# Weight-only products of two late stages computed at the start of the 16-head attention

## What is computed

```python
x = x + tanh(g_xattn[0]) * L0_xattn(ctx, ctx, layernorm(x))   # 16 heads of 16
x = x + tanh(g_ffn[0])   * L0_ffn(layernorm(x))               # 4 experts, each row to one
x = x + tanh(g_xattn[1]) * L1_xattn(layernorm(x), ctx, ctx)   # one head of 256
x = x + tanh(g_ffn[1])   * L1_ffn(layernorm(x))               # product-key memory

# L1_xattn: each of Q, K, V is a weight plus a product of rank 16
Q = query @ Q_weight.T + (query @ Q_A.T) @ Q_B.T
# L1_ffn: batch norm over all rows, queries, similarity with 2 x 8 x 64 keys, top 8
xn = (x - mu) * rsqrt(var + eps) * gamma + beta
sim = einsum(xn @ w_q.T, keys)
```

## Time and profile before

| | us |
|---|---|
| median of 3 runs | 3782.14 (3780.43 to 3783.98) |
| the profiled execution | 3779.93 |
| its span | 3778.3 |
| PE busy | 3467.6 (92%) |
| DVE busy | 2495.0 (66%) |
| ACT busy | 1560.8 (41%) |
| POOL busy | 226.7 (6%) |

### The profile page before, as it was taken

The page is one execution under the profiler, slowest core; times in us unless marked ns, Lnnn a source line. Parts: engine busy times, 40 slices in busy tenths (PEclk is TensorE's granted clock), DMA queues, the critical chain, the costliest instruction groups (busy, mean ns, idle before and its releaser), DMA issues. The chain is left out here.

```text
span 3778.3 us, 67015 instructions
## 1 busy us (share of the span) xinstructions
PE 3467.6 (92%) x21900; PEld 2037.8 (54%) x21900; DVE 2495.0 (66%) x5808; ACT 1560.8 (41%) x2718; POOL 226.7 (6%) x251
## 2 busy tenths in 40 slices
PE   8958999999999999867986999995999999999999
PEld 5631222222222222256873454544889888888898
DVE  4538877888788788461103344435888888888885
ACT  4525766767667677711221222211222222223221
POOL 0022000000000000020000000000000000000000
PEclk9978999999999999978997999996999999999999
DMA  5676445446445444051112122213000000000000
GB/s 218 229 210 96 61 68 79 60 66 81 60 69 72 67 63 57 5 189 48 38 51 78 46 91 64 64 40 147 9 12 10 11 12 10 11 10 11 12 10 9
DMA packets 144210, 240.30 MB, mean 64 GB/s; under 512 B 22808, under 2 KB 100224, under 8 KB 143488
## 3 DMA queue, kind: packets, MB, share of 16 engines
q1 hardware_dynamic: 134768, 220.67, 26.9%
q0 software_dynamic: 4608, 12.59, 1.0%
q10 hardware_dynamic: 4624, 4.46, 0.3%
HBM read 170.38 MB, written 66.86 MB: 63 GB/s over the span
## 5 line engine op out<-in xcount | busy, mean ns | idle before, releaser
L577 DVE TENSOR_REDUCE at_pmax<-at_psm 128x2 f32<-128x800 f32 (+1 forms) x1024 | 965.5, 988 | 257.9 <-PE at_psm L441 248.3
L531 ACT ACTIVATE at_pr<-at_pss 128x512 f32<-128x512 f32 (+1 forms) x1664 | 906.5, 598 | 332.8 <-PE at_pss L455 330.2
L455 PE MATMUL at_pss<-at_qs,at_ks 99*128 99x512 bf16 (+1 forms) x1664 | 584.4, 395 | 26.6 <-issue 19.5
L1632 PE MATMUL mt_psd<-mt_xl,mt_key_in 128*128 128x128 f32 x4096 | 492.0, 279 | 0.0
L1632 PEld LDWEIGHTS mt_psd<-mt_xl,mt_key_in 128*128 128x128 f32 x4096 | 470.6, 193 | 1.4
L463 PE MATMUL at_pso<-at_pr,at_vw 128*32 128x512 f32 (+1 forms) x3328 | 450.7, 613 | 0.0
L1658 PE MATMUL mt_psu<-mt_key_out,mt_g 128*128 128x256 f32 x2048 | 447.4, 379 | 1.3 <-DVE mt_g L1880 1.3
L455 PEld LDWEIGHTS at_pss<-at_qs,at_ks 99*128 99x128 bf16 (+1 forms) x1664 | 136.2, 98 | 560.9 <-ACT at_pr L531 408.2
L439 PE MATMUL at_psm<-at_ks,at_qs 64*128 64x400 bf16 (+1 forms) x1024 | 359.5, 351 | 75.4 <-DMA at_qs<-q_dram 35.7
L1658 PEld LDWEIGHTS mt_psu<-mt_key_out,mt_g 128*128 128x128 f32 x2048 | 386.7, 190 | 52.6 <-DVE mt_g L1880 1.4
L441 PE MATMUL at_psm<-at_kh,at_qh 64*128 64x400 bf16 (+1 forms) x1024 | 359.3, 351 | 0.0
(11 more groups left out here) (222 smaller groups left out, 3777.9 us busy)
## 6 DMA issues: line engine op xcount, KB each, us to landing
at_ks<-k_dram SPq DMA_DIRECT2D x192, 200.1 KB, 6.3
k_dram<-pj_kp SPq DMA_DIRECT2D x24, 800.5 KB, 5.4
v_dram<-pj_v SPq DMA_DIRECT2D x8, 1664.0 KB, 8.7
at_vd<-v_dram SPq DMA_DIRECT2D x32, 416.0 KB, 9.7
pj_ctx<-ctxT SPq DMA_DIRECT2D x8, 1601.0 KB, 11.3
at_kh<-k_dram SPq DMA_DIRECT2D x128, 100.1 KB, 5.4
aw_ctxT<-ctxT SPq DMA_DIRECT2D x8, 1601.0 KB, 7.1
at_qs<-q_dram SPq DMA_DIRECT2D x192, 64.0 KB, 6.5
```

Source lines behind the costliest of these rows:

```text
L455: nc.tensor.matmul(ps_s[0:r, (NST * g + n) % SBANKS, :], ks[:, g, j, kt * P:kt * P + r], qs[:, g, j, :], start=True, stop=True).then_inc(s ...
L531: nc.scalar.activation(pr[0:r, (NST * g + n) % PRING, :], ps_s[0:r, (NST * g + n) % SBANKS, :], ACT.Exp, scale=SCALE).then_inc(expd, 1)
L577: nc.vector.tensor_reduce(pmax[:, 2 * p:2 * p + 2, q, c:c + 1], ps_m[:, n % MBANKS, :, 0:MSPANS[c][1]], AX.X, ALU.max).then_inc(m_red, 1)
L1632: ins = nc.tensor.matmul(ps_d[:, j % 2, y * P:y * P + P], key_in[:, k, j * YB + y, :], xl[:, s, k, :], start=k == 0, stop=k == KC - 1)
```

## The change

- SP loads all weights concerned in `project`, behind the last context load and ahead of the last two batches' stores: 14 DMAs, 3.6 MB, on one semaphore.
- TensorE and VectorE do the mixing at the start of `attend_heads`, in the two banks of `ps_m`, and TensorE starts the second low-rank product without waiting for VectorE.
- The 32 key products stand one ahead of each of the first unit's 32 jobs; ScalarE copies them to `mk` in that stage.
- The weights use the space of `pr` (as `ring`) and of `acc`, `accT`, `den`, `o` (as `quad`), which are free until the first exponentials. `mk`, `gamma`, `beta`, `amat`, `cmat` stay in SBUF from there on.
- `attend_wide` and `memory` lose the loads, products and copies. In `memory`, TensorE waits for `ready` behind the first half scores, no longer ahead of the key products.

```diff
@@ -173,6 +173,15 @@
                         step(i, s, True)
+                sp.dma_start(t["w_keys"], t["m_wq_in"]).then_inc(t["weights_in"], 16)
+                sp.dma_start(t["keys"][:, :, :], t["m_keys_in"]).then_inc(t["weights_in"], 16)
+                sp.dma_start(t["gamma"][:, :], t["m_gamma_in"]).then_inc(t["weights_in"], 16)
+                sp.dma_start(t["beta"][:, :], t["m_beta_in"]).then_inc(t["weights_in"], 16)
+                for n, tile in t["wgt"].items():
+                    sp.dma_start(tile, t["l1_" + n + "_in"]).then_inc(t["weights_in"], 16)
+                for n, (left_, right) in t["low"].items():
+                    sp.dma_start(left_, t["l1_" + n + "a_in"]).then_inc(t["weights_in"], 16)
+                    sp.dma_start(right, t["l1_" + n + "bT_in"]).then_inc(t["weights_in"], 16)
@@ -346,15 +355,20 @@
         vw = st.sb("vw", [P, 2, KT * HG, 2 * DH])
-        pr = st.sb("pr", [P, PRING, S])
+        pr = t["ring"]
+        full = {n: st.sb(n + "f", [P, KC, D]) for n in "qkv"}
         pmax, nmax = st.sb("pmax", [P, HG, QT, NM]), st.sb("nmax", [P, HG * QT])
         mrest, mpart = st.sb("mrest", [HG * QT, 2, P]), st.sb("mpart", [HG * QT, 3, P], BF16)
-        acc, accT, den, o = st.sb("acc", [P, S]), st.sb("accT", [P, S // 32, 32]), st.sb("den", [P, S]), st.sb("o", [P, S])
+        acc, den, o = (t["quad"][:, i, :] for i in (0, 2, 3))
+        accT = t["quad"][:, 1, :].rearrange("p (b r) -> p b r", r=32)
         inv = st.sb("inv", [P, S // 32])
@@ -425,6 +439,43 @@
                 pe.sem_inc(pv, PRING)
+                def low_rank(n, name):
+                    if n == 2:
+                        pe.wait_ge(mixed_out, 1)
+                    left_, right = t["low"][name]
+                    for m in range(KC):
+                        ins = nc.tensor.matmul(ps_m[:, n % 2, m, 0:D], right[:, m * P:m * P + P], left_, start=True, stop=True)
+                    ins.then_inc(mixed, 1)
+                def mix(n, left_, right):
+                    pe.wait_ge(mixed_out, n)
+                    for m in range(KC):
+                        for k in range(KC):
+                            ins = nc.tensor.matmul(ps_m[:, n % 2, m, 0:D], left_[:, k, m * P:m * P + P], right[:, k, :],
+                                                   start=k == 0, stop=k == KC - 1)
+                    ins.then_inc(mixed, 1)
+                def key_product(i):
+                    n, h = i // MH, i % MH
+                    m, c = halves[n]
+                    if h == 0 and n >= SBANKS:
+                        pe.wait_ge(k_out, n - SBANKS + 1)
+                    ins = nc.tensor.matmul(ps_s[:, n % SBANKS, h * NK:(h + 1) * NK], t["w_keys"][:, c * MH + h, m * P:m * P + P],
+                                           t["keys"][:, c * MH + h, :], start=True, stop=True)
+                    if h == MH - 1:
+                        ins.then_inc(k_mm, 1)
+                pe.wait_ge(t["weights_in"], t["weights_n"])
+                low_rank(0, "q")
+                low_rank(1, "k")
+                low_rank(2, "v")
+                mix(3, full["q"], full["k"])
+                mix(4, full["v"], t["wgt"]["oT"])
+                pe.wait_ge(mixed_out, 5)
@@ -506,10 +557,12 @@
+                    key_product(n)
                     max_product(0, 0, 0, n)
                 turn_max(0)
                 for n in range(EARLY):
                     max_product(0, 1, 1, n)
+                pe.wait_ge(k_out, len(halves))
                 first_scores(0, 0)
                 with pe.Fori(0, last) as b:
@@ -521,6 +574,9 @@
+                for n, (m, c) in enumerate(halves):
+                    act.wait_ge(k_mm, n + 1)
+                    nc.scalar.activation(t["mk"][:, m, c * 512:c * 512 + 512], ps_s[:, n % SBANKS, :], ACT.Copy).then_inc(k_out, 1)
@@ -554,6 +610,12 @@
+                for n, name in enumerate("qkv"):
+                    dve.wait_ge(mixed, n + 1)
+                    nc.vector.tensor_tensor(full[name][:, :, :], ps_m[:, n % 2, :, 0:D], t["wgt"][name], ALU.add).then_inc(mixed_out, 1)
+                for n, dst in enumerate((t["amat"], t["cmat"])):
+                    dve.wait_ge(mixed, n + 4)
+                    nc.vector.tensor_copy(dst[:, :, :], ps_m[:, (n + 3) % 2, :, 0:D]).then_inc(mixed_out, 1)
@@ -1104,12 +1161,6 @@
-                for n in ("q", "k", "v", "oT"):
-                    sp.dma_start(wgt[n][:, :, :], t["l1_" + n + "_in"]).then_inc(w_in, 16)
-                for n in "qkv":
-                    sp.dma_start(low[n][0][:, :], t["l1_" + n + "a_in"]).then_inc(w_in, 16)
-                    sp.dma_start(low[n][1][:, :], t["l1_" + n + "bT_in"]).then_inc(w_in, 16)
@@ -1155,25 +1206,6 @@
             def _(pe):
-                pe.wait_ge(w_in, 160)
-                for n, name in enumerate("qkv"):
-                    if n:
-                        pe.wait_ge(mixed_out, n)
-                    for m in range(KC):
-                        ins = nc.tensor.matmul(ps_w[:, m, 0:D], low[name][1][:, m * P:m * P + P], low[name][0][:, :],
-                                               start=True, stop=True)
-                    ins.then_inc(mixed, 1)
-                for n, (left_, right) in enumerate(((full["q"], full["k"]), (full["v"], wgt["oT"]))):
-                    pe.wait_ge(mixed_out, 3 + n)
-                    for m in range(KC):
-                        for k in range(KC):
-                            ins = nc.tensor.matmul(ps_w[:, m, 0:D], left_[:, k, m * P:m * P + P], right[:, k, :],
-                                                   start=k == 0, stop=k == KC - 1)
-                    ins.then_inc(mixed, 1)
-                pe.wait_ge(mixed_out, 5)
@@ -1343,15 +1375,6 @@
-                dve.wait_ge(w_in, 160)
-                for n, name in enumerate("qkv"):
-                    dve.wait_ge(mixed, n + 1)
-                    nc.vector.tensor_tensor(full[name][:, :, :], ps_w[:, :, 0:D], wgt[name][:, :, :],
-                                            ALU.add).then_inc(mixed_out, 1)
-                for n, dst in enumerate((amat, cmat)):
-                    dve.wait_ge(mixed, n + 4)
-                    nc.vector.tensor_copy(dst[:, :, :], ps_w[:, :, 0:D]).then_inc(mixed_out, 1)
@@ -1525,8 +1544,6 @@
-                for dst, name in ((keys[:, :, :], "m_keys"), (wq, "m_wq"), (gamma[:, :], "m_gamma"), (beta[:, :], "m_beta")):
-                    sp.dma_start(dst, t[name + "_in"]).then_inc(mk_in, 16)
                 sp.dma_start(iota_f, t["m_iota_in"]).then_inc(iota_in, 16)
@@ -1589,7 +1606,6 @@
-                pe.wait_ge(ready, 1)
@@ -1660,18 +1676,10 @@
                 def first():
-                    pe.wait_ge(mk_in, 64)
-                    for n, (m, c) in enumerate(HALVES):
-                        if n > 1:
-                            pe.wait_ge(k_out, n - 1)
-                        for h in range(MH):
-                            ins = nc.tensor.matmul(ps_d[:, n % 2, h * NK:(h + 1) * NK], wq[:, c * MH + h, m * P:m * P + P],
-                                                   keys[:, c * MH + h, :], start=True, stop=True)
-                        ins.then_inc(k_mm, 1)
-                    pe.wait_ge(k_out, len(HALVES))
                     for off in range(2):
                         for c in range(2):
                             half_scores(0, off, c)
+                    pe.wait_ge(ready, 1)
@@ -1731,9 +1739,6 @@
-                    for n, (m, c) in enumerate(HALVES):
-                        act.wait_ge(k_mm, n + 1)
-                        nc.scalar.activation(mk[:, m, c * 512:c * 512 + 512], ps_d[:, n % 2, :], ACT.Copy).then_inc(k_out, 1)
@@ -1768,7 +1773,6 @@
                 dve.wait_ge(b_sd, 1)
-                dve.wait_ge(mk_in, 64)
@@ -1916,19 +1920,33 @@
+        mk = ctx.enter_context(nc.sbuf_tensor("mk", [P, KC, 2 * MH * NK], F32))
+        gamma = ctx.enter_context(nc.sbuf_tensor("gamma", [P, KC], F32))
+        beta = ctx.enter_context(nc.sbuf_tensor("beta", [P, KC], F32))
+        amat = x_life.enter_context(nc.sbuf_tensor("amat", [P, KC, D], F32))
+        cmat = x_life.enter_context(nc.sbuf_tensor("cmat", [P, KC, D], F32))
+        ring = stage_life.enter_context(nc.sbuf_tensor("ring", [P, 8, S], F32))
+        quad = stage_life.enter_context(nc.sbuf_tensor("quad", [P, 4, S], F32))
+        keys = stage_life.enter_context(nc.sbuf_tensor("keys", [P, 2 * MH, NK], F32))
+        low = stage_life.enter_context(nc.sbuf_tensor("low", [P, 2, D], F32))
+            "keys": keys, "w_keys": ring[:, :, :].rearrange("p (a b) n -> p a (b n)", b=1).rearrange("p a (c d) -> p (a c) d", d=D),
+            "wgt": {n: quad[:, i, :].rearrange("p (k d) -> p k d", d=D) for i, n in enumerate(("q", "k", "v", "oT"))},
+            "low": {n: (low[32 * i:32 * i + 16, 0, :], low[32 * i:32 * i + 16, 1, :]) for i, n in enumerate("qkv")},
@@ -1969,6 +1987,7 @@
         attend_heads(nc, sem, t)
+        stage_life.close()
         experts(nc, sem, t)
```

24 lines of the change are left out of this document (10 added, 14 removed).

## The result

| | us |
|---|---|
| before, median of 4 runs on the same chip | 3781.28 (3776.29 to 3783.98) |
| after, median of 4 runs | 3739.51 (3737.74 to 3741.73) |
| ratio, 95% interval | 0.989 (0.9876 to 0.9904) |
| profiled execution after, its span | 3741.73, 3740.1 |

The changed kernel is faster by 1.1%, 41.8 us by the medians and 38.2 us by the two profiled spans. The forecast was 33.5 us, 3748.6 us, and its range ended at 3741: right in sign and in which two stages pay, too slow by 9 us.

A forecast was written before the change was run, and what follows sets the result against it. All engines start each stage together, so a wait at its start was taken as paid in full. Gains 13.7 + 21.4 - 1.6 = 33.5 us off 3782.14 gave 3748.6 us, range 3741 to 3756.

The forecast's parts named there:

- Wide stage, 13.7 us: Start of wide attention: without loads and mixing, VectorE's addition waits only for the gather, 1987.5 for 2001.23; gain 13.7 us.
- the crowd's row: Wide stage: profile row of a fourth gather meeting context loads, packets still 6.7 us after issue; gives 1987.4, taken as 1987.5.
- the late end, 1989.6: Wide stage: gather packets alternate with large context packets, landing by 1989.6, gain 11.6 us; counted within the forecast's 0.82.
- Memory stage, 21.4 us: Start of memory stage: without key products and waits for their loads, scores start at 2570.7 for 2592.11; gain 21.4 us.
- the condition that the prediction had kept for its upper bound: Memory stage: TensorE at its high clock for the second half of the scores, giving the upper bound of 22.7 us.
- TensorE's own chain then caps it: Memory stage: with the second half of the scores at high clock, TensorE's own chain limits the gain to 22.7 us.
- Key products, 1.6 us lost: 16-head attention: 32 key products, one ahead of each pair of row-maxima products, cost 1.6 us, bounds 0 to 5.
- 0.435 against 0.38: Attention maxima: a key product takes 0.435 us, TensorE idles 0.38 us per period; 0.05 us left over, times 32.
- Mixing 0, loads 0: Mixing ends about 269.5, before the attention's operands land at 271.83; 14 loads fit idle DMA in the projection; both cost nothing.
- Moved work paid again: Rival, attention: mixing overruns 271.83, or each key product costs its whole 0.435 us, 13.9 us in all; 3761 us, chance 0.08.
- Loads hold up the stores: Rival, projection: the moved loads delay the stores behind them by all 8.5 us; 3757 us, chance 0.04.
- Clock stays low: Rival, wide and memory stages: chains starting cold run long at 0.50; 90 us of that gives 3794 us, chance 0.03.

The follow-up runs named there:

- second pair: Both kernels, before and changed, run once more unchanged for second traces and times: 3782.6 us before, 3743.05 us changed, ratio 0.9904.
- gathers_first: Changed kernel, with the wide stage's context loads held back until the four gathers of y have landed: median 3737.75 us.
- key_loads_early: Changed kernel, with the memory stage's key_in and key_out loads waiting for the first load of x only, not both: median 3740.4 us.
- loads_attention: Changed kernel, with its 14 weight loads issued at the start of the 16-head attention instead of in the projection: 3747.9 us, one run.
- mix_wide: Changed kernel, with the mixing and its loads back at the start of the wide attention, key products still moved: median 3756.7 us.
- keys_memory: Changed kernel, with key products, their loads and the wait for ready back in the memory stage, mixing still moved: median 3767.9 us.
- pad_behind: Kernel before, with four small unused ScalarE copies added at the start of the wide attention, behind the experts: 3781.8 us, one run.

## Why the forecast was too slow

*Wide stage, 13.7 us.* Right: the addition is 14.0 us nearer to the opening (13.75 in the second pair of traces), and the choice of the crowd's row was right for its reason: alone the gather takes 2.7 us (gathers_first), in the crowd 6.65, and the prediction had read 6.7 from the row. Of the 14.0, 13.35 arrive at the next stage. The Trainium skill, "DMA: Bandwidth & Descriptors" (Queues, rings and completion order), has each DMA engine take its queues in turn, a packet of each. The trace agrees that the gather shares the engines with its neighbours (6.65 against 2.7 us), but the late end, 1989.6, which the prediction put to this rule, did not occur: the gather was in at 1987.0.

*Memory stage, 21.4 us.* This is the term that was mis-sized: 24.6 us, above the upper bound of 22.7. The mechanism was right (scores at 4.15 us, dense start waiting for key_out). Three numbers were not. The landing of key_out was taken from the earlier trace rows, 23.6 us, the longest of the eighteen traces; in the others the load takes 21.5 to 22.7 us, 22.3 in the changed kernel. So the dense start moved by 21.6 us and not by 20.0. VectorE's chain, which the prediction shifts by 21.4 us as TensorE's scores, moved by 23.5, because the second scores ran at 1.00: the condition that the prediction had kept for its upper bound came true. And the step that failed is "TensorE's own chain then caps it" at 22.7. With the 21.6, with the 2.74 us of wait that disappears, and less 1.2 us by which TensorE's work from there to the picks got longer (dense products 17.20 us, 16.62 before; the wait for xb 4.84, 4.42 before; the scores 3.77, 3.43 before), the picks move by 23.2 us (79.07 behind the opening, now 55.91). And because TensorE no longer stops there, the dense products behind take 3.84 us in place of 5.22: 1.4 us more, which no term held. key_loads_early, which brings the stop back, brings the 5.19 us back.

*Key products, 1.6 us lost.* 5.2 at the turn, above the upper bound of 5, and with the rest of the change some 4 at the first exp. The step "0.435 against 0.38" failed: 0.435 us is the price of a key product in a row of such products. Between products of another shape it takes 0.62 us (272.13 to 272.75 above) and the pair 0.44, 1.06 together, over VectorE's 0.90. That TensorE is the bound here is a matter of its clock: for the three jobs at 1.00 in loads_attention the same order costs nothing.

*Mixing 0, loads 0.* Right (mix_wide, loads_attention); the mixing was done 14.8 us behind the opening, 16.3 in the prediction. 0.5 us went at the end of the projection by something else.

*What the forecast did not have.* 3.8 us in the experts, in a stage that the diff does not touch, by the place of a loop in ScalarE's program: the prediction takes only the three places that the diff touches, and so puts every other stage at nothing. With it the parts add up to 13.35 + 24.6 - 4 - 0.5 + 3.8 = 37.2 us; the two pairs of medians gave 41.8 and 35.6. The forecast's 33.5 is 3.7 less than the parts. That is the experts' 3.8; of the rest, the memory stage's gain of 3.2 over the forecast and the attention's loss of 2.4 over it, with the 0.5 and 0.35 of the wide stage, cancel. The 4.6 us from 37.2 to the first 41.8 are not shown to be the change's: the second pair lies 1.6 below 37.2, all times together give 40.2, and the dip in the projection (2.35 us) and the loop (12 us from the shortest to the longest) vary by as much. That the measured time fell just outside the range is therefore in part the scatter of four runs; the memory stage above its bound and the missing 3.8 us are not.

*The rivals.* Moved work paid again: in part, 5.2 in place of 13.9. Loads hold up the stores: no. Clock stays low: no; the starts of the stages ran at 0.50 for a few microseconds as before, and the second scores of the memory stage at 1.00. The Trainium skill, "TensorE: Matmul & The Clock Gate" (Part 1: The HAM clock gate), says that the low clock is the default and that activity releases it, from which the prediction drew that products taken away make the next ones slow. Here that did not show: the memory stage lost 13.9 us of products ahead of its scores and its second scores ran at 1.00, where they ran at 0.50 before.

## What to carry over

Where a stage opens with weight-only work and an earlier stage has a hole on the same engines, moving it can pay nearly its whole length, and more where its loads held up others: here 13.35 of some 17 us of mixing, and 24.6 us for 13.9 us of key products and the waits for their loads. Look for the hole by the longest idle of the engine ahead of a block, and put the moved products where they stand alone, not between products on the engine that is near its limit at its lower clock. Take the duration of a single load from more than one trace: one of 23.6 us, 1.3 more than in the changed kernel, made most of an error of 1.6 us. And compare stage by stage, opening to opening, before a difference of medians is put down to a change: the four columns of the table repeat within 0.7 us, where the gain by medians wandered by 6. An instruction that is slow once, always at the same place, is worth a query for what the instruction queue did just then.

## What the runs showed of the hardware

The first store that ScalarE issues in a loop took 2.3 us or 0.46 us depending on two small copies with their waits ahead of it in ScalarE's program, and over the 18 traces it went with the program without an exception: 2.2 to 2.4 us in four (before twice, keys_memory, pad_behind), 0.46 or less in fourteen. In the four, an 8 KB packet of the instruction queue q14 starts 0.66 to 0.69 us into the issue; in the fourteen it starts 2.5 to 8.1 us ahead of it. One such issue cost 3.8 us: 1.98 us of idle TensorE and about as much by its clock behind that.

The granted clock made the same block of 32 key products last 7.36 us in one trace and 13.92 in the other, with the same work ahead of it. In the projection the second block of products took 7.3 to 8.7 us in thirteen traces, with 0.50 in it and TensorE idle for 2.65 to 3.76 us ahead, and 5.81 us in five, at 1.00, with 2.16 to 2.36 us idle; both kinds of kernel are in both sets. Products behind such a wait ran at 0.50 for a while, so that the wait had a second price: some 1.8 us behind the 1.98 us in the experts, 1.35 us behind the 2.78 us at the turned picks.
